# Two attention layers over four batches: first heads' slots filled from SBUF, products moved into the fills

## The chip, the cores and the metric

The kernel runs on one core of one Trainium2 chip. The metric is the device time of one execution in microseconds (us), as the median of several runs of the same program on the same inputs.

## What is computed

Two cross-attention layers run one after the other on `x` (4 batches, 512 queries, 320 channels) and a context `ctx` (4 batches, 512 tokens, 512 features), with 20 heads of width 16. In the first layer each head attends to the first 77 tokens (`text`) and to the other 435 (`ip`) with weights and softmaxes of their own. In the second layer the text is the first 508 tokens and `ip` the last 4, and the scores on the 4 tokens get a cosine between the averaged context `qsem` and each of the 4 tokens.

```
# first layer, each head
out = softmax(q k_text^T * s) v_text + softmax(q k_ip^T * s) v_ip
x = out @ Wo^T + bo + x
# second layer, each head
probs = softmax(q k_text^T * s)
qsem = l2norm(probs @ text);  sem = qsem @ l2norm(ip)^T
probs_ip = softmax(q k_ip^T * s + 0.5 * sem) * mask
x = (probs @ v_text + probs_ip @ v_ip) @ W_out + b_out + x
```

## The kernel before

Every engine runs a program of its own; counting semaphores join them, and nothing schedules but the order in which the code is written. A batch has four stages: the first layer's heads, a stretch of products between the layers, the second layer's heads, a stretch of products before the next batch. Batches 0, 1 and 2 are one `Fori` loop (`run_batches`), batch 3 is written out behind it, so there are two jumps back, at the ends of batches 0 and 1.

**Products.** `JOBS` lists the products of the stretches. Each goes to one PSUM bank of a ring of four (`ps_s`, `ps_t`), and ScalarE ("A") or VectorE ("D") frees it. Into the second layer they are `k1`, `tr0` (heads' outputs transposed), `x1` (output projection and residual), `q1`, then `g` (four blocks of `ctx^T ctx`, the Gram matrix from which `qsem`'s norm comes) and `v1` (four blocks of values). Into the next first layer they are `k0`, `q0`, `v0t` and `v0i` (values), `tr1` and `y` (output and residual).

**Slots.** Keys and queries go to TensorE in two parts, high and low, to keep fp32 accuracy. ScalarE's `high` and VectorE's `low` write the parts to SBUF, SyncE's `store` writes them to DRAM (`parts_k`, `parts_q`), and `load_slots` reads each head back, 48 rows at a time, into one of four slots (`k_slot`, `q_slot`). `split_and_loaded` does all that for one layer: it waits for all three row blocks of `k` and stores them, the same for `q`, waits until all is stored, and loads heads 0 to 3, then 4 to 19 as slots come free.

**Heads.** `run_heads` is a pipeline of three heads. `step(n)` makes the scores of head n+2 with their maxima, the transposed scores and exponentials of head n+1, and uses those of head n. Steps -2 and -1 are the fill: they have no head to use, so each hand-over (scores on TensorE, maximum on VectorE, bias on GpSimd, exponential on ScalarE) is waited for. The second layer's `step1` multiplies each head's exponentials with the Gram matrix (`ps_w<-gram,...`); before its step 0 TensorE waits for the copies in `before_use`, and ScalarE issues the next batch's loads (`context_done`).

## Time and profile before

| | us |
|---|---|
| median of three runs | 1805.31 (1803.68 to 1805.6) |
| the profiled execution | 1810.82 |
| its span, first to last instruction | 1809.0 |
| TensorE busy in the span | 1635.4 |
| VectorE, ScalarE, GpSimd busy | 1272.7, 1116.1, 463.6 |
| mean granted TensorE clock | 0.96 of full |

In the profile, times of instructions are counted from the span's start. Busy matmul time includes the tail of each matmul, which overlaps the next. The granted clock is 1.0 or 0.5 of full speed at any moment.

### The profile page before, as it was taken

The numbers are of one execution on the slowest core, as the hardware profiler recorded it, in microseconds if no ns is written. First come the engines' busy times: TensorE is split into PE (matmuls) and PEld (weight loads), VectorE is DVE, ScalarE is ACT, GpSimd is POOL, SyncE is SP. The second block draws the span as 40 slices with busy tenths as digits, with TensorE's granted clock in tenths as the row PEclk, the third lists the DMA queues.
The fourth block names the chain that finished last, engine by engine and source line by source line (L and its number), as shares of the span: only waits on it lengthen the run. The fifth ranks groups of instructions, "written<-read, shape, count | busy, mean of one in ns | idle before, by whom it ended". The sixth has DMA issues, their size and how long they took to land.

```text
span 1809.0 us, 34075 instructions
## 1 busy us (share of the span) xinstructions
PE 1635.4 (90%) x8608; PEld 1234.2 (68%) x8608; DVE 1272.7 (70%) x3548; ACT 1116.1 (62%) x2323; POOL 463.6 (26%) x1225
## 2 busy tenths in 40 slices
PE   5788989999978898999988888999998889999993
PEld 2455469999445447999835544999974554799991
DVE  2487358887678717888758853788875883588875
ACT  1599157776279627777429943677734991577760
POOL 0244013232025302323104411222301540233220
PEclk9899989999989998999989999999998999899996
DMA  7210220000301031001030111100012102100000
GB/s 234 75 35 22 88 65 21 19 18 20 114 29 35 13 104 53 22 17 32 1 121 31 35 48 61 59 20 17 28 45 85 35 26 79 36 18 21 17 20 15
DMA packets 47284, 83.04 MB, mean 46 GB/s; under 512 B 4417, under 2 KB 11857, under 8 KB 47185
## 3 DMA queue, kind: packets, MB, share of 16 engines
q1 hardware_dynamic: 43040, 74.15, 12.5%
q10 hardware_dynamic: 4144, 7.76, 1.4%
q8 instruction: 40, 0.66, 0.2%
q14 instruction: 60, 0.48, 0.1%
HBM read 47.78 MB, written 34.10 MB: 45 GB/s over the span
## 4 chain that ended last, share of the span: by engine, by line
PE 77%; ACT 10%; issue 5%; DVE 5%; DMA 1%; POOL 1%; ACTq 1%; SPq 0%; POOLq 0%; DVEq 0%
PE ps_w L838 37%; PE ps_s L838 17%; PE ps_t L838 16%; PE ps_b L838 4%; ACT probsT_high L461 4%; ACT probsT L469 4%; DVE row_max L648 2%; PE ps_m L838 2%; ACT q_slot L454 1%; ACT probs L495 1%; POOL probsT_low L383 1%; ACT probs L478 0%; ACT probs L536 0%; DMA w_ki<-in_wki 0%; DVE row_max L679 0%
## 5 line engine op out<-in xcount | busy, mean ns | idle before, releaser
L637 DVE TENSOR_TENSOR probsT_low<-probsT,probsT_high 128x512 fp32r<-128x512 f32 x560 | 394.1, 704 | 85.2 <-ACT probsT L469 76.0
L461 ACT ACTIVATE probsT_high<-ps_t 128x512 fp32r<-128x512 f32 x640 | 382.6, 598 | 113.9 <-PE ps_t L838 109.9
L838 PE MATMUL ps_w<-gram,probsT_high 128*128 128x416 f32 (+2 forms) x1280 | 390.8, 316 | 0.0
L469 ACT ACTIVATE probsT<-ps_t 128x512 f32<-128x512 f32 x640 | 384.0, 600 | 0.0
L838 PE MATMUL ps_w<-gram_low,probsT_high 128*128 128x384 f32 (+2 forms) x1280 | 354.5, 305 | 0.0
L495 ACT ACTIVATE probs<-ps_s,exp_bias 128x508 f32<-128x508 f32 x320 | 220.9, 691 | 125.9 <-POOL exp_bias L394 82.6
L838 PE MATMUL ps_s<-k_slot,q_slot 96*128 96x512 f32 x640 | 249.6, 434 | 32.0 <-issue 13.0
L838 PE MATMUL ps_t<-q_slot,k_slot 98*128 98x512 f32 x640 | 266.1, 435 | 11.0 <-ACT q_slot L454 9.2
L394 POOL TENSOR_SCALAR exp_bias<-row_max 128x1 f32<-128x1 f32 x320 | 129.7, 405 | 551.8 <-DVE row_max L679 551.8
L838 PEld LDWEIGHTS ps_w<-gram_low,probsT_high 128*128 128x128 f32 (+1 forms) x1280 | 244.8, 191 | 11.1
L838 PEld LDWEIGHTS ps_w<-gram,probsT_high 128*128 128x128 f32 (+1 forms) x1280 | 243.2, 190 | 11.5
L838 PE MATMUL ps_w<-gram,probsT_low 128*128 128x400 f32 (+2 forms) x1280 | 247.0, 315 | 0.0
L679 DVE TENSOR_REDUCE row_max<-ps_s 128x1 fp32r<-128x508 f32 x320 | 216.4, 677 | 0.0
L838 PEld LDWEIGHTS ps_w<-gram,probsT_low 128*128 128x128 f32 (+1 forms) x1280 | 214.4, 191 | 0.0
L696 DVE CUSTOM_DVE_ANT_0 probs<-ps_w,probs 128x380 f32<-128x380 f32 x320 | 174.0, 544 | 0.0
L648 DVE TENSOR_REDUCE row_max<-ps_s 128x2 fp32r<-128x870 f32 x160 | 168.2, 1051 | 0.0
L838 PEld LDWEIGHTS ps_t<-q_slot,k_slot 98*128 98x128 f32 x640 | 124.6, 196 | 58.3 <-ACT probsT L469 22.5
L838 PEld LDWEIGHTS ps_s<-k_slot,q_slot 96*128 96x128 f32 x640 | 119.7, 200 | 65.0 <-issue 28.0
L383 POOL TENSOR_TENSOR probsT_low<-probsT,probsT_high 128x512 fp32r<-128x512 f32 x80 | 103.6, 1295 | 164.2 <-ACT probsT L469 164.2
L454 ACT ACTIVATE q_slot<-ps_m 2x512 fp32r<-2x512 f32 x160 | 93.7, 586 | 79.1 <-PE ps_m L838 67.3
L695 DVE COPY head_out<-ps_w 128x36 f32<-128x36 f32 x320 | 62.3, 195 | 103.7 <-PE ps_w L838 103.6
L371 POOL CAST v_slot<-v_sb 128x16 fp32r (+3 forms) x160 | 63.8, 431 | 278.6 <-ACT probs L478 125.1
(153 smaller groups left out, 2056.9 us busy)
## 6 DMA issues: line engine op xcount, KB each, us to landing
q_slot<-parts_q SPq DMA_DIRECT2D x160, 96.0 KB
k_slot<-parts_k SPq DMA_DIRECT2D x160, 96.0 KB
parts_k<-probsT_high SPq DMA_DIRECT2D x24, 512.0 KB, 4.2
parts_q<-probsT_low SPq DMA_DIRECT2D x24, 512.0 KB, 4.3
parts_k<-probsT_high SPq DMA_DIRECT2D x24, 128.0 KB, 3.8
parts_q<-probsT_low SPq DMA_DIRECT2D x24, 128.0 KB, 3.6
ctx_sb<-in_ctxT ACTq DMA_DIRECT2D x3, 1024.0 KB, 8.3
vip_rep<-vip_rows SPq DMA_DIRECT2D x16, 160.0 KB, 3.6
```

Source lines behind the costliest of these rows:

```text
L371: last = nc.gpsimd.tensor_copy(v0_slot[par][:, blocks, cols], src)
L383: nc.gpsimd.tensor_tensor(probsT_low[1 - par][:, TB - 1, :], probsT[:, TB - 1, :], probsT_high[1 - par][:, TB - 1, :].bitcast(F32), ALU.su ...
L394: nc.gpsimd.tensor_scalar_mul(exp_bias[par][:, c:c + 1], row_max[1][par][:, c, 0:1].bitcast(F32), -SCALE)\
L454: nc.scalar.activation(q_slot[(k + 1) % SLOTS][SHIFT_ROW:ALL_ROWS, :], ps_m[0:SHIFT_ROWS, :], ACT.Copy)\
L461: nc.scalar.activation(probsT_high[1 - par][:, t, :], ps_t[:, t % 2, :], ACT.Exp, scale=SCALE)
L469: nc.scalar.activation(probsT[:, t, :], ps_t[:, t % 2, :], ACT.Exp, scale=SCALE).then_inc(pt_block[l], 1)
L495: nc.scalar.activation(probs[par][:, c, 0:TEXT1], ps_s[:, c % 2, 0:TEXT1], ACT.Exp, bias=exp_bias[par][:, c:c + 1], scale=SCALE, accum_out ...
L637: nc.vector.tensor_tensor(probsT_low[1 - par][:, t, :], probsT[:, t, :], probsT_high[1 - par][:, t, :].bitcast(F32), ALU.subtract).then_in ...
L648: nc.vector.tensor_reduce(out=row_max[0][par][:, cs, SHIFT_ROWS - 1:SHIFT_ROWS], in_=ps_s[:, :, TEXT0:T], axis=AX.X, op=ALU.max).then_inc( ...
L679: nc.vector.tensor_reduce(out=row_max[1][par][:, c, 0:1], in_=ps_s[:, c % 2, 0:TEXT1], axis=AX.X, op=ALU.max).then_inc(max_chunk, 1)
L696: nc.vector.tensor_tensor_reduce(out=probs[par][:, c, P:TEXT1], in0=ps_w[c % 2][:, 0:GN], in1=probs[par][:, c, P:TEXT1], scale=1.0, scalar ...
L838: return nc.tensor.matmul(out, lhsT, rhs, start=start, stop=stop)
```

## The change

In `split_and_loaded`, SyncE handles each row block by itself: as soon as row block 0 of `k` or `q` (the channels of heads 0 to 7) is split, twelve DMAs of 16 rows copy the parts of heads 0 to 3 from SBUF into the slots (`first_heads`), then the blocks are stored one by one. Only heads 4 to 19 are read from DRAM. `q1`'s parts get buffers of their own (`x_sb` and `out_all`), since `probsT_low` is written in the fill; for the first layer ScalarE and VectorE wait in step -1 for the stores of `k0` and `q0` instead.

On TensorE, the products `g` and `v1` stand inside the second layer's fill. Those of `v0t`, `v0i`, `tr1` and `y` stand inside the next first layer's fill (`fill0`), which is now at the end of a batch, ahead of the jump back. These products use a second ring, `ps_w0`, `ps_w1`, `ps_b`. The copies on ScalarE and VectorE move with them, GpSimd prepares head 0's values behind the fill (`gram_ready`), and SyncE instead of ScalarE issues the stores of the outputs.

```diff
+LATE = [("g", i) for i in range(TB)] + [("v1", t) for t in range(TB)] + [("ipn", 0), ("vip", 0)]
+BETWEEN = [("v0t", 0)] + [("v0i", t) for t in range(TB)] + [("tr1", m) for m in range(CBN)] + [("y", m) for m in range(CBN)]
...
+RING_NEXT = {("k0", 0): 2, ("k0", 1): 3, ("k0", 2): 0, ("q0", 0): 1, ("q0", 1): 2, ("q0", 2): 3}
+RING_BEFORE = {("q0", 1): ("k0", 0), ("q0", 2): ("k0", 1)}
...
+        parts["q1"] = [x_sb[:, :, :].bitcast(F32R),
+                       out_all[:, 0:CBN * S].rearrange("p (k s) -> p k s", k=CBN).bitcast(F32R)]
...
+        late_ring = [ps_w[0][:, :], ps_w[1][:, :], ps_b[:, :]]
+        late = {job: late_ring[i % len(late_ring)] for i, job in enumerate(LATE)}
+        late.update({job: late_ring[i % len(late_ring)] for i, job in enumerate(BETWEEN)})
...
+        def fill0(step, batch, b=FIRST):
+
+
+
+            step(batch, -2, SLOTS - 2, -1, False, False, True, b)
+            step(batch, -1, SLOTS - 1, -1, False, True, True, b)
+
+        def run_heads0(step, eng, b):
+
+            with eng.Fori(0, TURNS - 1) as turn:
+                for k in range(SLOTS):
+                    step(b, SLOTS * turn + k, k, turn, True, True, True)
+            for k in range(SLOTS):
+                step(b, HEADS - SLOTS + k, k, TURNS - 1, True, k < SLOTS - 1, k < SLOTS - 2)
...
-            def store(b, name):
+            def store(name, m):
                 for i, part in enumerate(ROW_PARTS[name[0]]):
-                    dst = scratch[name][i, :, :, :].rearrange("h d s -> (h d) s")
-                    src = parts[name][part].bitcast(F32)
-                    sp.dma_start(dst[0:2 * P, :].rearrange("(k p) s -> p k s", p=P), src[:, 0:2, :]).then_inc(stored[name], 16)
-                    sp.dma_start(dst[2 * P:C, :], src[0:CB[2], 2, :]).then_inc(stored[name], 16)
+                    dst = scratch[name][i, :, :, :].rearrange("h d s -> (h d) s")[P * m:P * m + CB[m], :]
+                    sp.dma_start(dst, parts[name][part].bitcast(F32)[0:CB[m], m, :]).then_inc(stored[name], 16)
+
+            def first_heads(l, name):
+
+                for k in range(SLOTS):
+                    slot = (q_slot if name[0] == "q" else k_slot)[k]
+                    for i, part in enumerate(ROW_PARTS[name[0]]):
+                        sp.dma_start(slot[PART * i:PART * i + PART, :].bitcast(F32),
+                                     parts[name][part].bitcast(F32)[D * k:D * k + D, 0, :]).then_inc(slots_in[l][k], 16)
...
-            def load_all(b, l):
-                with sp.Fori(0, TURNS) as turn:
-                    for k in range(SLOTS):
-                        load_slots(b, l, SLOTS * turn + k, k)
-
             def split_and_loaded(b, batch, l, names):
                 for name in names:
-                    wait_freed(sp, b, name, CBN - 1)
-                    store(b, name)
+                    for m in range(CBN):
+                        wait_freed(sp, b, name, m)
+                        sp.sem_inc(passed, 1)
+                        if m == 0:
+                            first_heads(l, name)
+                        store(name, m)
+                if l == 0 and b is not FIRST:
+                    store_outputs(b)
                 for name in names:
                     sp.wait_ge(stored[name], STORES * (batch + 1))
                 sp.sem_inc(passed, 1)
-                load_all(batch, l)
+                with sp.Fori(0, TURNS - 1) as turn:
+                    for k in range(SLOTS):
+                        load_slots(batch, l, SLOTS * turn + SLOTS + k, k)
+
+            def store_outputs(b):
+                for m in range(CBN):
+                    wait_freed(sp, b, "y", m)
+                    sp.sem_inc(passed, 1)
+                    sp.dma_start(outT[b, m * P:m * P + CB[m], :], x1_sb[0:CB[m], m, :]).then_inc(y_out, 16)
...
+                run_heads0(step0, pool, b)
+                def gram_ready():
+
+                    pool.wait_ge(stored["q1"], STORES * (b + 1))
+                    wait_freed(pool, b, "v1", TB - 1)
+                    pool.sem_inc(passed, 1)
+                    values_of(b, 0, 0)
+                    wait_freed(pool, b, "g", TB - 1)
+                    pool.sem_inc(passed, 1)
+                    for i in range(TB):
+                        lo = P * max(i, 1) - P
+                        nc.gpsimd.tensor_copy(gram[1][:, i, lo:GA], gram[0][:, i, lo:GA])
+                    values_of(b, 1, 1)
+
+                run_heads(step1, pool, b, gram_ready)
...
+                if transposed and not use:
+                    act.wait_ge(stored["k0"], STORES * (b + 1))
...
+                first, second = not use and not transposed, not use and transposed
                 if transposed:
                     shift(b, 1, n, k)
+                if second:
+                    gram_rows(b, 2)
+                    act.wait_ge(stored["k1"], STORES * (b + 1))
                 for c in range(SC):
                     if transposed:
                         expT(b, 1, n, par, c)
                     if scores and c < 2:
                         exps(c)
+                    if second and c == 0:
+                        gram_rows(b, 3)
+                    if second and c < TB - 1:
+                        v1_rows(b, c)
+                if first:
+                    gram_rows(b, 0)
                 if scores:
                     exps(2)
                     exps(3)
+                if first:
+                    gram_rows(b, 1)
+                if second:
+                    v1_rows(b, 3)
...
 
                 if scores:
                     maxima(0)
+                if outputs:
+                    output(last, 0)
+                if transposed and not use:
+                    dve.wait_ge(stored["q0"], STORES * (b + 1))
                 if transposed:
                     lowT(b, 0, n, par, 0)
                 if scores:
                     maxima(1)
+                if outputs:
+                    output(last, 1)
                 if transposed:
                     lowT(b, 0, n, par, 1)
+                if outputs:
+                    output(last, 2)
                 if use:
 
                     dve.wait_ge(o_done, HEADS * b + n + 1)
...
+                first, second = not use and not transposed, not use and transposed
+                output = second and last is not FIRST
                 if scores:
                     scores_half(0)
+                if first:
+                    values0(last)
+                if output:
+                    wait_freed(pe, last, "tr1", CBN - 1)
+                    by_channels(last, "y", "o1", heads_outT, (0,))
...
                     scoresT_of(0, g, k, 1)
+                if output:
+                    by_channels(last, "y", "o1", heads_outT, (1,))
...
+                if output:
+                    by_channels(last, "y", "o1", heads_outT, (2,))
+                if first and last is not FIRST:
+                    transposed_heads(last, "tr1", 1)
                 if scores:
```

**TensorE, into the second layer.** These are the last block of `q1` and what follows it, before the change (`ps_t<-x_sb,w_q` is `q1`, `<-ctx_sb` alone is `g`, `w_v` is `v1`, `k_slot,q_slot` are scores).

```order
L838 MATMUL ps_t<-x_sb,w_q 64x512 x3
L838 MATMUL ps_s<-ctx_sb 128x512 x4
L242 REGISTER_ALU
L838 MATMUL ps_s<-ctx_sb 128x384 x4
L242 REGISTER_ALU
L838 MATMUL ps_t<-ctx_sb 128x256 x4
L242 REGISTER_ALU
L838 MATMUL ps_t<-ctx_sb 128x128 x4
L242 REGISTER_ALU
L838 MATMUL ps_s<-w_v,ctx_sb 128x320 x4
```

The same place on TensorE after the change:

```order
L931 MATMUL ps_t<-x_sb,w_q 64x512 x3
L978 REGISTER_ALU
L1087 ISA
L931 MATMUL ps_s<-k_slot,q_slot 128x512
L1087 REGISTER_ALU
L931 MATMUL ps_s<-k_slot,q_slot 128x512
L931 MATMUL ps_w<-ctx_sb 128x512 x4
L1087 REGISTER_ALU
L931 MATMUL ps_s<-k_slot,q_slot 128x512
L1087 REGISTER_ALU
L931 MATMUL ps_s<-k_slot,q_slot 128x512
L931 MATMUL ps_w<-ctx_sb 128x384 x4
```

The scores of head 0 come directly behind `q1`, and the Gram blocks between them; the value blocks follow in step -1 in the same way.

**TensorE, into the next first layer.** These are the end of `q0` (`x_sb,w_q`) and the rows up to the jump back: `w_v` and `w_vi` are values, `ident,probsT` is `tr1`, `probs,w_o` is `y`.

```order
L838 MATMUL ps_t<-x_sb,w_q 64x512 x3
L242 REGISTER_ALU
L838 MATMUL ps_s<-w_v,ctx_sb 77x320 x4
L242 REGISTER_ALU
L838 MATMUL ps_s<-w_vi,ctx_sb 128x320 x4
...
L838 MATMUL ps_s<-probs,w_o 128x512 x3
...
L838 MATMUL ps_t<-probs,w_o 64x512 x3
L242 REGISTER_ALU
L252 REGISTER_ALU
L252 COMPARE_AND_BRANCH
L838 MATMUL ps_s<-k_slot,q_slot 128x512 x4
L838 MATMUL ps_m<-ident_r,row_max 2x128 x4
```

The same place on TensorE after the change:

```order
L931 MATMUL ps_t<-x_sb,w_q 64x512 x3
...
L995 ISA
L931 MATMUL ps_s<-k_slot,q_slot 128x512 x2
L931 MATMUL ps_w<-w_v,ctx_sb 77x320 x4
L931 MATMUL ps_w<-w_vi,ctx_sb 128x320 x4
...
L931 MATMUL ps_s<-k_slot,q_slot 128x512 x2
...
L1194 MATMUL ps_b<-ident,probsT 128x128 x4
...
L931 MATMUL ps_b<-probs,w_o 128x512 x3
...
L931 MATMUL ps_t<-q_slot,k_slot 128x512
...
L931 MATMUL ps_w<-probs,w_o 128x512 x3
...
L931 MATMUL ps_w<-probs,w_o 64x512 x3
...
L263 COMPARE_AND_BRANCH
```

The scores of the new batch's first heads stand ahead of the values, the transposes and outputs stand between them, and the jump comes behind the fill.

**SyncE, into the next first layer.** These are the stores and loads between the second layer's last load and the first layer's loop of loads.

```order
L312 DMA parts_k<-probsT_high 128x2x512
L313 DMA parts_k<-probsT_high 64x512
...
L312 DMA parts_q<-probsT_low 128x2x512
L313 DMA parts_q<-probsT_low 64x512
...
L334 ISA
...
L321 DMA q_slot<-parts_q 48x1x512
L321 DMA k_slot<-parts_k 48x1x512
```

The same place on SyncE after the change:

```order
L344 DMA k_slot<-probsT_high 16x512 x12
L337 DMA parts_k<-probsT_high 128x512 x3
...
L344 DMA q_slot<-probsT_low 16x512 x12
L337 DMA parts_q<-probsT_low 128x512 x3
...
L377 DMA outT<-x_sb 128x512
...
L367 ISA
...
L351 ISA
L353 ISA
```

The copies to the slots stand ahead of each name's stores, so `q`'s first copy comes behind 21 issues for `k`; the stores of the output stand ahead of the wait for `parts_k` and `parts_q`.

## Rows read from the trace of the kernel before

**Rows 1.** Windows: us, busy time per engine, PEclk, DMA share, GB/s.

```profile
682.00:690.00 8.00, 6.90 (x21) 4.29 (x22) 5.62 (x13) 6.29 (x15) 1.77 (x5) 0.53 0.00 0
705.00:865.00 160.00, 160.00 (x1055) 153.38 (x1054) 136.04 (x496) 120.12 (x266) 48.35 (x152) 1.00 0.07 22
965.00:1000.00 35.00, 30.15 (x153) 18.90 (x152) 31.43 (x52) 33.19 (x64) 17.23 (x32) 1.00 0.11 36
```

**Rows 2.** Timeline, TensorE, a steady second-layer head: start, length, [idle before <- what ended it].

```profile
701.49 1.10 PE L838 MATMUL ps_b<-gram,probsT 128*128 128x128 f32 x8
...
704.47 0.44 PE L838 MATMUL ps_t<-q_slot,k_slot 98*128 98x512 f32 x1
```

**Rows 3.** Timeline, TensorE, first to second layer, batch 1.

```profile
656.25 6.28 PE L838 MATMUL ps_s<-ctx_sb 128*128 128x512 f32 x16
...
674.37 0.73 PE L838 MATMUL ps_s<-k_slot,q_slot 96*128 96x512 f32 x2 [0.60 <-ACT v_sb L551]
...
681.89 0.50 PE L838 MATMUL ps_t<-q_slot,k_slot 98*128 98x512 f32 x1 [1.42 <-ACT q_slot L454]
...
687.46 2.07 PE L838 MATMUL ps_b<-gram,probsT 128*128 128x128 f32 x8
...
694.12 0.50 PE L838 MATMUL ps_t<-q_slot,k_slot 98*128 98x512 f32 x1 [1.01 <-ACT q_slot L454]
```

**Rows 4.** Timeline, TensorE, first to second layer, last batch.

```profile
1548.47 0.73 PE L838 MATMUL ps_s<-k_slot,q_slot 96*128 96x512 f32 x2 [0.53 <-ACT v_sb L551]
...
1566.84 0.44 PE L838 MATMUL ps_t<-q_slot,k_slot 98*128 98x512 f32 x1
```

**Rows 5.** Timeline, TensorE, into the next first layer, batches 1 to 2.

```profile
914.02 2.38 PE L838 MATMUL ps_s<-w_v,ctx_sb 128*77 128x320 f32 x8
...
927.17 6.00 PE L838 MATMUL ps_s<-probs,w_o 128*128 128x512 f32 x12 [0.85 <-ACT probs L536]
...
941.08 1.21 PE L838 MATMUL ps_s<-k_slot,q_slot 96*128 96x512 f32 x2 [5.05 <-issue]
...
952.19 1.22 PE L838 MATMUL ps_s<-k_slot,q_slot 96*128 96x512 f32 x2
...
958.85 0.72 PE L838 MATMUL ps_s<-k_slot,q_slot 96*128 96x512 f32 x2
```

**Rows 6.** Timeline, TensorE, into the last batch, whose code is unrolled.

```profile
1377.35 0.70 PE L838 MATMUL ps_s<-k_slot,q_slot 96*128 96x512 f32 x2 [1.16 <-DVE x_sb L818]
...
1395.10 0.71 PE L838 MATMUL ps_s<-k_slot,q_slot 96*128 96x512 f32 x2
```

**Rows 7.** Timeline, VectorE, batches 1 to 2.

```profile
898.55 0.69 DVE L631 TENSOR_TENSOR probsT_high<-ps_t,probsT_high 128x512 fp32r<-128x512 f32 x1 [0.74 <-ACT probsT_high L448]
...
911.53 0.68 DVE L631 TENSOR_TENSOR probsT_low<-ps_s,probsT_low 128x512 fp32r<-128x512 f32 x1
...
922.96 1.49 DVE L815 TENSOR_TENSOR probsT<-probs 128x1280 f32<-128x1280 f32 x1
```

**Rows 8.** Tile k_slot, SyncE queue: issues, ns min/median/max; then us to landing.

```profile
L321 SPq DMA_DIRECT2D k_slot<-parts_k x160: 713/722/802, 55.1 to 1719.1; - x160
L291 SPq DMA_DIRECT2D k_slot<-ip_shift x4: 574/586/667, 8.8 to 10.8; - x4
...
DMA to landing us min/median/max: 1.7/1.7/1.8
```

**Rows 9.** Tile parts_q: 64-row store issues, ns; us to landing.

```profile
L313 SPq DMA_DIRECT2D parts_q<-probsT_low x24: 479/495/1242, 46.2 to 1536.0; - x24
...
DMA to landing us min/median/max: 2.9/4.0/4.9
```

**Rows 10.** Timeline, SyncE queue, start of the program.

```profile
35.24 0.59 SPq L306 DMA_DIRECT2D mask_sb<-in_mask  x1
```

**Rows 11.** Timeline, TensorE, first fill.

```profile
44.29 2.38 PE L838 MATMUL ps_s<-w_v,ctx_sb 128*77 128x320 f32 x8
...
78.01 0.71 PE L838 MATMUL ps_s<-k_slot,q_slot 96*128 96x512 f32 x2
```

More of the change, by code:

```diff
@@ L360, in _, with step0 @@
                                     pattern=[[-1, P]], channel_multiplier=1).then_inc(built, 1)
[L362 removed]
+            def step0(b, n, k, turn, use, transposed, scores, last=FIRST):
                 par = k % 2
@@ L704, in step1 @@
                         maxima(c)
-                    if not use and not transposed and c == 1:
-                        ip_context(b)
+                    if first and c % 2 == 1:
+                        gram_lows(b, c // 2)
                     if use and c == 3:
@@ L823, in batch @@
                     link(b, nc.vector.memset(dump[:, 8:9], 0.0))
+                if ahead:
+                    fill0(step0, b + 1, b)
+                else:
+                    for m in range(CBN):
+                        output(b, m)
             lows(FIRST, "k0")
             lows(FIRST, "q0")
+            fill0(step0, 0)
             run_batches(dve, batch)
@@ L885, in head_maxT, with step0 @@
                 last.then_inc(maxT_done[l], 1)
-            def step0(b, n, k, turn, use, transposed, scores):
+            def step0(b, n, k, turn, use, transposed, scores, last=FIRST):
                 par = k % 2
@@ L974, in scores_of @@
                     scores_chunk((k + 2) % SLOTS, c, ps_s[:, c % 2, :]).then_inc(s_chunk, 1)
+                first, second = not use and not transposed, not use and transposed
                 if use:
@@ L998, in step1 @@
                     scores_of(1)
-                if not use and not transposed:
-                    ip_context(b)
+                if first:
+                    gram_of_context(b, 0)
+                if second:
+                    by_keys(b, "v1", "v1", 1)
                 if use:
```

186 lines of the change are left out of this document (106 added, 80 removed).

## The prediction, as put on record

> **What bounds the kernel now.** I read the windows first, then TensorE's timeline through each stretch between two layers, then the queues that feed it. In the middle of the second layer TensorE is busy 160.00 of 160 us, at the full clock (2.4 GHz); in the first layer's heads it is busy 30.15 of 35 us, the rest being short waits for other engines [rows 1]. The change touches neither: the same matmuls stand in every head. What it can move is the stretches around the fills. In the one into the second layer, products on the context run from 656.25 to 674.37, then the fill goes from 674.37 to 687.46, with idle times of which one of 1.42 is shown, and the granted clock is 0.53 from 682 to 690, so nearly all of that at the lower level, 1.2 GHz [rows 1, 3]. In the one into the next first layer, TensorE sits idle 5.05 us with nothing to wait for in the profile ("issue") before the first scores [rows 5]. That idle time is at the jump back of the batch loop: where the code is unrolled, at the last batch, it is 1.16 us, and ends with VectorE's output copy [rows 6]. So some 4 us of it belong to the jump; I use 4.3, as the output copy ends 0.75 us behind the last matmul, at 936.8.
>
> **Into the second layer, four times.** The products (17.5 us net of the last wait) and the fill are now one piece. Before, the fill took 687.46 - 674.37 = 13.1 us [rows 3]. I take 3.7 us of it as idle (the 1.42 shown, the rest smaller waits for maxima and exponentials) and half of the 3.9 us of matmuls at the low clock behind 682, 1.9 us, as lost to the clock; 7.5 us are work. The product blocks, of 1 to 3.5 us each, now stand in each of those waits. One wait is new: head 0 needs TensorE's last `vip` product copied, about 0.7 us. That makes 656.25 + 17.5 + 7.5 + 0.7 = 682.0 for the start of step 0, against 687.46. From there a steady head takes 704.47 - 701.49 = 3.0 us to its first transposed scores [rows 2]; before, at the low clock, it took 694.12 - 687.46 = 6.7, 1.01 of it waiting for ScalarE, which was still issuing the next batch's loads [rows 3]. ScalarE's queue issues them at the same place, so I keep 1.0: the scores come at 686.0, 8.1 us earlier. The last batch has no loads to issue: there the same piece took 1566.84 - 1548.47 = 18.4 us instead of 19.75, without the wait, so it gains 8.1 - 1.4 + 1.0 = 7.7 [rows 3, 4]. Four stretches: 3 x 8.1 + 7.7 = 32.0. Bounds: with only the 3.7 + 1.9 us of waiting and clock in the fill halved and the low clock kept in head 0, 3 us each (12); with no wait for ScalarE at all, 9 us each (36).
>
> ScalarE and VectorE get the Gram and value copies into a place where they were mostly waiting. GpSimd waits for `q1`'s stores behind the fill, some 15 us after their last issue, against landings of 2.9 to 4.9 us [rows 9], so that costs nothing. If the stores were later than that, the wait would hold head 0's values and TensorE with them.
>
> **What the slots cost.** The scores can start only when 16-row copies from SBUF have landed, and these stand in SyncE's one queue. None is in the trace. The nearest issues: a single row from SBUF to a slot takes 586 ns at the median, a 64-row store 495, a 48-row load from DRAM 722 [rows 8, 9]. I take 0.6 us, near the single row, which has the same source and target. Landing: the single row 1.7 us, a store 4.0 at the median [rows 8, 9]; I take 2.0, since source and target are those of the single row. [...] With 4.0 us instead, each fill that waits for its slot loses 2 us more.
>
> Into the second layer `k1` is long stored when `q1` comes, and the first queries' three issues and landing (1.8 + 2.0) fit in `q1`'s last two blocks of 3 us each. Into the next first layer it is closer. `k0`'s first block is split at 898.55 + 0.69 = 899.2; 12 copies and 9 stores at 0.6 keep the queue to 911.8; `q0`'s first block is split at 912.2, since VectorE has it between long operations [rows 7]; three issues and the landing give 916.0. TensorE has ended `q0` at 914.02 [rows 5]. It waits 2.0 us, and everything in its queue with it: the values, the transposes, the outputs.
>
> **Into the next first layer, batches 0 and 1.** Without that wait, values, transposes and outputs take from 914.02 to 941.08 - 5.05 = 936.0 [rows 5], of which 0.85 before the output is a wait that the fill now covers: 21.1 us. The fill's own work at the full clock is 12 score matmuls and 8 small ones, about 4.6 us; 1.3 us for waits of maxima and the last output copy. 914.0 + 2.0 + 21.1 + 4.6 + 1.3 = 943.0. VectorE's chain ends with 922.96 + 1.49 = 924.45 [rows 7] and serves the first maxima before TensorE has ended the values, so it doesn't hold. Then comes the jump, 4.3 us, not hidden by anything since all engines stand at it: step 0 starts at 947.3, against 952.19 [rows 5]. Before, the low clock that followed the idle time lay on the fill and the start of step 0, which took 958.85 - 952.19 = 6.7 us instead of about 5.4. Now it lies on steps full of matmuls, where half the clock costs more: I charge 3.5 us (0 if the clock holds, 7 if it is low for three heads). Gain: 4.9 + 1.3 - 3.5 = 2.7 us, twice, 5.4. Bounds of one: -3 to +7.
>
> **Into the last batch.** No jump: 943.0 is 6.2 us later than the last output copy before (936.8), which there ends at about 1377.1, just ahead of the first scores, so the heads can start at 1383.3. Before, step 1 started at 1395.10, so step 0 at the full clock would have begun at 1389.7 [rows 6]. That is 6.4; I take 5.5, for some low clock after the 2 us wait.
>
> **The first fill.** SyncE is busy with weight loads until 35.24 + 0.59 = 35.8 [rows 10]. 21 issues give 48.4, three more and the landing 52.2. TensorE has ended `q0` at 44.29 [rows 11], so it sits idle 7.9 us, then does the values (some 11 of the 12.3 us up to the output's wait in the later stretch [rows 5], part of it at the low clock) and the fill: step 1 starts near 81.5, against 78.01 [rows 11]: -3.5. Bounds: -8 to 0.
>
> **Sum.** 32.0 + 5.4 + 5.5 - 3.5 = 39.4 us off. The profiled execution took 1810.8 us, its span 1809.0; the median of the runs, 1805.3, is 0.3% lower, and I apply the sum to it: 1766 us. What moved at no cost is the issue of the outputs' stores from ScalarE to SyncE: they stand in front of SyncE's wait for the stores and of head 4's load, and that head's scores come two heads, 11 us, later.
>
> **Rivals.**
> - *Slower issues* (or landings): at 0.72 us for each 16-row copy and store, the 24 issues from `k0` to the first slot end 2.9 us later, against 0.4 us of room. With three such fills and 3 to 4 us at the first, 12 us are lost: 1778. A landing of 4.0 us does 8 of that alone.
> - *Other side:* the same queue, from about 1.0 us an issue. Then each of four fills loses 24 x 0.4 = 10 us, and the 39 us are gone. The longest 64-row store took 1242 ns [rows 9]; if all issues took that, each fill would lose 24 x 0.64 = 15 us, and the time would be about 1827. Medians of 586 ns for one row and 495 for 64 rows speak against it [rows 8, 9].
> - *The low clock stays.* The 2 us wait for the queries comes in an otherwise full piece. The granted clock fell to half in 682 to 690 after idle times of this size [rows 1, 3]. If it falls here, 5 us are lost on the values and again behind the jump: three times 5 to 6, 1782. The Trainium skill, "TensorE: Matmul & The Clock Gate", section "Loop structure matters more than you think", warns of just this: a DMA wait in front of matmuls lets the clock drop. By it the last two cases would come together.
> - *No gain into the second layer*: the hand-overs on ScalarE, now with 12 copies more, set the fill's pace. Then the four stretches gain 3 us each, and the sum is 19: 1786. A first-layer head already keeps ScalarE at 33.19 of 35 us [rows 1], so it has little room in a steady stage; but in the fill the 17.5 us of products give it time for twelve copies that are smaller than its exponentials.
>
> **Chances.** The forecast 0.60 (1755 to 1774); the queue at 0.72 or the landing 0.13 (1774 to 1782); clock or ScalarE 0.16 (1778 to 1795); the queue from 1.0 us on, 0.04; all waits hidden, under 1755, 0.07. The range that leaves out no more than 2 in 10 is 1754 to 1787. Differences below 0.2% can't be told from none; within that I put 0.02, slower 0.04, faster 0.94.
>
> **What would show it.** In the changed profile: TensorE's first Gram product of a second layer some 26 us behind `q1` and a clock of 1.00 through it; first scores of a first layer about 2 us behind `q0`, ended by a landing; 16-row issues near 0.6 us; an idle time of 4 to 5 us behind the last maximum's transposes in batches 0 and 1 alone, with a low clock on the heads behind it. I am wrong if those issues take 1 us, if the products leave idle times between them, or if heads slow down elsewhere.

## The result, and the profile after

Four runs of each kernel on the same chip gave 1753.99 us (1752.99 to 1755.05) against 1804.49 us (1803.60 to 1805.60): a ratio of 0.972, 95% interval 0.970 to 0.974. That is 50.5 us off, where the forecast was 39.4. The profiled execution of before (1810.82 us) isn't among its four; that of after (1753.93 us) is. The sign and the mechanism held; the gains into both layers were put too small.

The page of the changed kernel, its head, and below it the windows (us, then busy time of each engine, granted clock, DMA share, GB/s) that answer to [rows 1] and to the two kinds of fill:

```profile
span 1752.1 us, 34255 instructions
PE 1601.0 (91%) x8608; PEld 1218.5 (70%) x8608; DVE 1271.6 (73%) x3548; ACT 1113.8 (64%) x2323; POOL 461.3 (26%) x1225
```

```profile
630.00:667.00 37.00, 35.08 (x121) 18.54 (x119) 14.03 (x34) 15.55 (x40) 4.94 (x18) 1.00 0.23 71
667.00:682.00 15.00, 15.00 (x103) 14.45 (x104) 11.22 (x46) 9.37 (x20) 3.25 (x11) 1.00 0.39 128
705.00:865.00 160.00, 160.00 (x1061) 153.69 (x1060) 134.31 (x496) 116.78 (x257) 47.58 (x151) 1.00 0.06 19
889.00:918.00 29.00, 27.19 (x92) 14.37 (x90) 19.14 (x34) 8.16 (x16) 1.65 (x8) 0.94 0.33 102
918.00:931.00 13.00, 7.58 (x31) 4.89 (x30) 5.75 (x10) 6.35 (x12) 2.62 (x5) 0.74 0.14 38
```

Read the head first. The same 8608 matmuls keep TensorE busy 34.4 us less than the 1635.4 us of before, out of 56.9 us by which the two profiled spans differ. The other 22.5 us are idle time. Most of the 34 us is clock: in the low stretches of the two traces TensorE was busy for 96.4 us before and for 33.5 after. A score matmul of 0.40 us (682.23 before) took 0.79 there (686.82), so half of the difference, 31 us, is an estimate of what the clock gave back. The remaining 3 us may be tails of matmuls, which overlap more when the matmuls stand closer; that isn't shown. The mean granted clock agrees: 0.96 leaves 0.04 x 2 x 1809.0 = 145 us at the lower level, 0.981 leaves 67. The second layer's fill and its start (630 to 682) are at 1.00 throughout; before, 682 to 690 had 0.53 [rows 1].

TensorE's timeline of the changed kernel, into the second layer of batch 1, answers to [rows 3]:

```profile
636.10 5.90 PE L931 MATMUL ps_t<-x_sb,w_q 128*128 128x512 f32 x12
641.92 0.74 PE L931 MATMUL ps_s<-k_slot,q_slot 96*128 96x512 f32 x2
642.50 3.60 PE L931 MATMUL ps_w<-ctx_sb 128*128 128x512 f32 x8
...
666.86 1.15 PE L931 MATMUL ps_b<-gram,probsT 128*128 128x128 f32 x8 [1.08 <-DVE vip L823]
...
669.89 0.44 PE L931 MATMUL ps_t<-q_slot,k_slot 98*128 98x512 f32 x1
```

Scores start with no wait behind `q1`: the slots have landed. From `q1`'s end to head 0's first transposed scores it now takes 669.89 - 641.92 = 27.97 us, and took 694.12 - 656.25 = 37.87: 9.9 us less, forecast 8.1. ScalarE's timeline at that place shows why head 0 no longer waits for it:

```profile
666.80 0.41 ACTq L297 DMA_DIRECT2D ctx_sb<-in_ctxT  x1
...
667.92 0.54 ACTq L301 DMA_DIRECT2D x_sb<-in_xT  x1
668.72 0.58 ACT L507 ACTIVATE q_slot<-ps_m 2x512 fp32r<-2x512 f32 x1 [5.48 <-PE ps_m L931]
```

Its three load issues begin at 666.80, just ahead of step 0 (666.86), and end at 668.46, before the shift row is wanted. Before the change they stood behind the last exponentials of the fill. They began 2.9 us behind step 0's start (687.46) and took 2.8 us:

```profile
690.38 0.43 ACTq L271 DMA_DIRECT2D ctx_sb<-in_ctxT  x1
...
690.97 1.23 ACTq L274 DMA_DIRECT2D x_sb<-in_xT  x1
692.36 0.79 ACTq L275 DMA_DIRECT2D x_sb<-in_xT  x1
693.41 0.58 ACT L454 ACTIVATE q_slot<-ps_m 2x512 fp32r<-2x512 f32 x1 [2.80 <-issue]
```

TensorE's timeline into the first layer of batch 2 answers to [rows 5], and SyncE's issues at the same place to [rows 8, 9]:

```profile
888.71 1.07 PE L931 MATMUL ps_t<-x_sb,w_q 64*64 64x512 f32 x2
891.52 0.72 PE L931 MATMUL ps_s<-k_slot,q_slot 96*128 96x512 f32 x2 [1.74 <-DMA q_slot<-probsT_low]
892.08 3.55 PE L931 MATMUL ps_w<-w_v,ctx_sb 128*77 128x320 f32 x8
...
917.69 0.40 PE L931 MATMUL ps_m<-ident_r,row_max 128*2 128x128 f32 x4
922.83 1.22 PE L931 MATMUL ps_s<-k_slot,q_slot 96*128 96x512 f32 x2 [4.74 <-issue]
...
929.91 0.71 PE L931 MATMUL ps_s<-k_slot,q_slot 96*128 96x512 f32 x2
```

```profile
875.70 6.94 SPq L344 DMA_DIRECT2D k_slot<-probsT_high  x11
882.68 5.34 SPq L337 DMA_DIRECT2D parts_k<-probsT_high  x9
888.20 8.28 SPq L344 DMA_DIRECT2D q_slot<-probsT_low  x12
```

The copies take SyncE 0.63 to 0.69 us from one to the next (forecast 0.6), the stores 0.59. The wait for the queries is 1.74 us here and in the last batch, 1.97 in batch 1 (forecast 2.0), the jump back 4.74 (forecast 4.3). In the very first fill the wait is 9.11 us (forecast 7.9) and step 1 starts at 80.42 (forecast 81.5, before 78.01 [rows 11]):

```profile
52.87 1.22 PE L931 MATMUL ps_s<-k_slot,q_slot 96*128 96x512 f32 x2 [9.11 <-DMA q_slot<-probsT_low]
```

To compare kernels I cut the trace at step 0's first transposed scores and at each layer's end; "first step 0" is the time of these scores in batch 0's first layer. "Into second layer" is from a first layer's end to the second layer's step 0; "into first layer" from a second layer's end to the next step 0. From the traces, in us:

| kernel | first step 0 | into second layer, batches 0 to 3 | into first layer, three |
|---|---|---|---|
| before | 73.5 | 71.2, 72.8, 72.9, 69.6 | 60.7, 60.5, 56.0 |
| after | 76.0 | 62.9, 61.3, 61.3, 61.1 | 54.1, 55.4, 50.7 |
| e1 first side ahead | 76.1 | 61.4, 61.3, 62.9, 61.1 | 59.4, 60.0, 56.1 |
| e2 second side ahead | 76.1 | 75.7, 75.7, 75.7, 73.7 | 54.1, 53.7, 49.4 |
| e3 slots alone | 70.6 | 74.5, 74.0, 73.6, 73.5 | 59.7, 60.0, 56.1 |
| e4 slots from DRAM | 79.4 | 73.9, 74.7, 76.1, 74.8 | 67.2, 67.2, 62.6 |
| e5 second side, products put right | 76.4 | 73.0, 74.4, 74.4, 72.3 | 55.6, 55.4, 50.7 |
| e6 slots alone, products put right | 70.4 | 73.2, 74.3, 72.9, 72.6 | 59.7, 59.3, 55.6 |
| e9 slots alone, cleanly | 70.1 | 71.1, 71.7, 72.2, 68.3 | 59.2, 59.8, 56.0 |
| e13 second side, cleanly | 75.9 | 71.4, 72.2, 72.2, 71.3 | 53.9, 53.9, 49.0 |
| e10 before, with filler | 73.1 | 74.2, 72.7, 72.2, 70.3 | 60.3, 60.3, 55.6 |
| e7 unrolled | 75.2 | 61.1, 61.1, 61.1, 61.1 | 50.8, 48.8, 48.8 |
| e8 queries first | 71.4 | 61.3, 61.3, 61.3, 61.2 | 53.9, 53.4, 48.7 |
| e11 both | 71.3 | 61.1, 61.1, 61.1, 61.1 | 48.6, 48.6, 48.5 |
| e12 values split | 70.5 | 61.1, 61.1, 61.1, 62.8 | 47.9, 47.9, 47.9 |

### The profile page after: what moved, and what is told of

Its sections match the earlier page's. It is cut to its first block, busy times and chain, and to the rows that moved or that the text cites. A ratio compares the mean times of both kernels' runs of the same rounds, so it can differ in the third digit from the quotient of the medians.

```text
span 1752.1 us, 34255 instructions
## 1 busy us (share of the span) xinstructions
PE 1601.0 (91%) x8608; PEld 1218.5 (70%) x8608; DVE 1271.6 (73%) x3548; ACT 1113.8 (64%) x2323; POOL 461.3 (26%) x1225
## 4 chain that ended last, share of the span: by engine, by line
PE 75%; ACT 9%; issue 7%; SPq 4%; DVE 3%; POOL 1%; DMA 0%; ACTq 0%; POOLq 0%; DVEq 0%
PE ps_w L931 44%; PE ps_t L931 11%; PE ps_s L931 11%; PE ps_b L931 7%; ACT probsT_high L514 4%; ACT probsT L522 4%; DVE row_max L725 2%; SPq L344 2%; PE ps_m L931 2%; SPq L337 1%; SPq L309 1%; ACT probs L533 1%; POOL probsT_low L425 1%; PE ps_b L1058 0%; DMA q_slot<-probsT_low 0%
## 5 line engine op out<-in xcount | busy, mean ns | idle before, releaser
L706 DVE TENSOR_TENSOR probsT_low<-probsT,probsT_high 128x512 fp32r<-128x512 f32 x560 | 393.1, 702 | 83.5 <-ACT probsT L522 74.2
L931 PE MATMUL ps_s<-k_slot,q_slot 96*128 96x512 f32 x640 | 240.3, 418 | 29.9 <-DMA q_slot<-probsT_low 14.6
L931 PE MATMUL ps_t<-q_slot,k_slot 98*128 98x512 f32 x640 | 262.2, 427 | 1.0
L931 PE MATMUL ps_w<-probsT_high,v_slot 128*68 128x512 f32 x320 | 107.4, 416 | 9.1 <-ACT probsT L522 4.5
```

What stands on the lines that cost most here:

```text
L706: nc.vector.tensor_tensor(probsT_low[1 - par][:, t, :], probsT[:, t, :], probsT_high[1 - par][:, t, :].bitcast(F32), ALU.subtract).then_in ...
L931: return nc.tensor.matmul(out, lhsT, rhs, start=start, stop=stop)
```

## Experiments: which half brings it

The theory: products cover the fills' waits and so keep the clock up, and the copies from SBUF are what lets the first scores stand ahead of the products. The rivals: the copies alone bring it; the order alone brings it; or it is the clock alone. The runs were made on several chips, and the kernel before took 1806 to 1809 us beside them, so ratios to it (with 95% intervals) are compared, not times alone.

**e1.** The first layer's side undone. The edit on TensorE (VectorE's three outputs stand ahead of its fill likewise):

```diff
                 if ahead:
+                    values0(b)
+                transposed_heads(b, "tr1", 1)
+                wait_freed(pe, b, "tr1", CBN - 1)
+                by_channels(b, "y", "o1", heads_outT)
+                if ahead:
+                    wait_freed(pe, b, "y", CBN - 1)
                     fill0(step0, b + 1, b)
-                    wait_freed(pe, b, "y", CBN - 1)
-                else:
-                    transposed_heads(b, "tr1", 1)
-                    wait_freed(pe, b, "tr1", CBN - 1)
-                    by_channels(b, "y", "o1", heads_outT)
```

> The changed kernel with one part undone: values, transposed heads and outputs stand ahead of the next first layer's fill again, as in the kernel before; the very first fill and all second-layer fills stay changed. My theory (the products cover the waits of the fill): the stretches into the next first layer take what they took before, less nothing for the slots, since the copies from SBUF land behind products either way. They gained 6.6, 5.1 and 5.3 us with the heads' +1.6, +0.7, -1.1 beside them, so 14 to 17 us come back: 1768 to 1771. Rival, slots alone: if the gain there came from slots that are filled sooner, it stays and the time is 1754 to 1757. Rival, low clock: if moving the products only moved a low-clock stretch, under 5 us come back, 1755 to 1759.

Measured 1775.16 us, 0.983 (0.981 to 0.985): 1.1% of the time, some 20 us, comes back, a little more than expected. The three stretches take 59.4, 60.0 and 56.1 us, against 60.7, 60.5 and 56.0 before. The slots alone bring 1.3 us at most there.

**e2.** The second layer's side undone:

```diff
                 by_channels(b, "q1", "q1", x1_sb)
+                for i in range(TB):
+                    gram_of_context(b, i)
+                for t in range(TB):
+                    by_keys(b, "v1", "v1", t)
+                wait_freed(pe, b, "v1", TB - 1)
```

with the same calls taken out of `step1`, ScalarE's and VectorE's copies moved along, and the four-bank ring of before.

> The changed kernel with the other part undone: Gram and value products of the second layer stand ahead of its fill again, ip_context in its last step; the first-layer side stays changed. My theory: the four stretches into the second layer, 62.9, 61.3, 61.3, 61.1 us in the changed kernel, go back to 70 to 73 each, 32 to 42 us in all: 1786 to 1796. I expect ScalarE's wait for its load issues (1.0 us) and the low clock of the fill to come back with it. Rival, slots alone: the gain came from copying the first slots out of SBUF, and the time stays within 1754 to 1760.

Measured 1806.18, 1.000 (0.999 to 1.001): 50 to 52 us come back, not 32 to 42, and the stretches are 2.8 to 4.5 us longer than in the kernel before. So e2 had lost something that before had (e5, e13).

**e3.** e1 and e2 together, and the values ahead of the very first fill too.

> Only the SBUF copies of the first four heads are left of the change: all products stand ahead of the fills, in the first layer's first fill too. My theory: in the kernel before, no fill waited for a DMA except the very first one, so this is the time of before less what the first fill gains (2 to 5 us): 1798 to 1804. Rival, slots alone bring the gain: 1754 to 1770. Rival, the queue: 24 issues on SyncE in one piece delay the heads behind them, over 1806.

Measured 1814.25, 1.005 (1.003 to 1.007): slower than expected, and in the range of the queue rival. But the stretches into the first layer are at most 0.1 us longer than before; it is those into the second that are, by 0.7 to 3.9 us, as in e2. What that is, e5, e6 and e9 ask.

**e4.** The changed order with the first slots from DRAM:

```diff
-                        if m == 0:
-                            first_heads(l, name)
...
                 sp.sem_inc(passed, 1)
+                for k in range(SLOTS):
+                    load_slots(batch, l, k, k)
```

> The changed kernel's order of products with the slots of heads 0 to 3 filled from DRAM again, behind the stores. With e3 this makes the two-by-two table of copies and order. My theory: both parts need each other. The first scores stand ahead of the products and wait for nine stores, their landing (2.9 us), a load issue and its landing (2.5 us): 9 us more at three first-layer fills, 5 to 7 at four second-layer fills, 2 at the first: 45 to 57 us more, 1800 to 1811, so no gain over before is left. Rival, order alone: the products cover the round trip, 1754 to 1765.

Measured 1848.21, 1.024 (1.022 to 1.026). The direction is right, the size nearly double (94 us over the changed kernel). Its TensorE timeline into the second layer and into the next first one:

```profile
680.81 1.22 PE L931 MATMUL ps_s<-k_slot,q_slot 96*128 96x512 f32 x2 [11.04 <-DMA k_slot<-parts_k]
...
943.99 1.21 PE L931 MATMUL ps_s<-k_slot,q_slot 96*128 96x512 f32 x2 [13.02 <-DMA k_slot<-parts_k]
```

I had expected 5 to 7 and 9 us. The waits come with low clock behind them: TensorE's busy time is 1614.5 us against 1601.0. The order alone is worse than nothing. (The nine stores of a name take SyncE 5.3 us, the six of before took 4.6, so storing block by block isn't the cause.)

**e5, e6.** The kernels e2 and e3 had kept the two image-prompt products at the end of step -1, where nothing covers them any more. Here they are back in step -2:

```diff
                     scores_of(1)
                 if first:
-                    gram_of_context(b, 0)
-                if second:
-                    by_keys(b, "v1", "v1", 1)
+                    ip_context(b)
...
-                if second:
-                    by_keys(b, "v1", "v1", 3)
-                    ip_context(b)
```

> e2 again with one thing put right: e2 had left the two image-prompt products (norms and values of the last four context rows) at the end of step -1, where nothing covers them once the Gram products stand ahead; here they are back in step -2, between its second and third score block, as in the kernel before. My theory: e2's stretches into the second layer (75.7 us) held 3 to 4 us of that each, so they come to 72 to 73 us, and the time to 1790 to 1797, 36 to 43 us over the changed kernel. Rival: the place of the two products costs nothing and e2's 1806 stands, so that the waits of the changed SyncE and GpSimd queues cost it.

> e3 again with the image-prompt products in step -2 as in the kernel before, so that only the SBUF copies of the first four heads (and the buffers that they need) are left of the change. My theory: stretches into the second layer as before (70 to 73 us), into the next first layer 0.4 to 1.0 us shorter, first fill 2.4 us shorter as in e3: 1798 to 1803, a change of 0.1 to 0.4%. Rival, the copies cost what they bring: 1805 to 1810.

Measured 1807.01, 0.999 (0.998 to 1.000), and 1815.61, 1.005 (1.003 to 1.006). e5 is its rival; e6 lies even above its own. The stretches into the second layer fell by 1.3 to 2.7 us from e2 to e5, but the whole did not, since those into the first layer came out 1.3 to 1.7 us longer; no run says why. They are still 1.5 to 2.7 us above the kernel before. TensorE's timeline of e6 shows one thing that was missing, a wait that the products had covered:

```profile
688.46 0.74 PE L919 MATMUL ps_m<-ident_r,row_max 128*2 128x128 f32 x4
691.34 0.71 PE L919 MATMUL ps_w<-gram,probsT_high 128*128 128x416 f32 x1 [2.13 <-POOL gram L434]
```

In the changed kernel GpSimd splits head 0's values behind the fill. There TensorE doesn't wait for them; here, without products in the fill, it does.

**e9, e13.** So GpSimd's order of before goes with it:

```diff
-                if use and scores:
+                if scores:
                     values_of(b, n + 2, par)
...
-                    values_of(b, 0, 0)
...
-                    values_of(b, 1, 1)
```

> e6 once more with GpSimd's order of before as well: the Gram copies ahead of the fill and the two first heads' value splits within it, where e6 still had them behind it, so that TensorE waited 2.13 us for the first head's values in each second layer. Now only the copies from SBUF and their buffers are left. My theory: e6's into-second-layer stretches (73.0 to 74.3 us) lose 2 us each, and the time comes to 0.995 to 1.000 of the kernel before (1796 to 1805 where that takes 1805): the copies alone are worth only the first fill's 2 to 3 us. Rival, the copies' 24 issues on SyncE cost what they bring: 1.002 to 1.005.

> The changed kernel with the second layer's side undone cleanly: Gram and value products ahead of the fill, the two image-prompt products in step -2, and GpSimd's Gram copies and value splits where the kernel before has them (e5 had them behind the fill, with a wait of 2 us on TensorE). My theory: the products in the second layer's fills are worth what e9 and the changed kernel differ by in these four stretches, 8.2, 10.4, 10.9 and 7.2 us, 37 us in all, plus up to 2 us of low clock in the heads behind them: 1790 to 1794, a ratio to the kernel before of 0.990 to 0.993. Rival, e5 stands: the wait for GpSimd only hid another one, 0.997 to 1.000.

e9: 1806.22, 0.999 (0.998 to 1.000), as expected. e13: 1797.43 (1791.46 to 1800.15), 0.995 (0.993 to 0.997), slightly above what I had expected, and under the rival; its profiled execution, the fastest of six, has a span of 1789.7 us, 37.6 over the changed kernel's. From e6 to e9 the four stretches fell by 2.1, 2.6, 0.7 and 4.3 us, from e5 to e13 by 1.6, 2.2, 2.2 and 1.0. This gives a clean table, in ratios to the kernel before:

| | products ahead of fills | products in the fills |
|---|---|---|
| first slots from DRAM | 1 | 1.024 (e4) |
| first slots from SBUF | 0.999 (e9) | 0.972 |

Neither half brings anything alone. e9 also keeps the smaller parts of the change (stores block by block, `q1`'s own buffers, SyncE storing the outputs), so none of these is the gain. The products in the second layer's fills are worth 40.5 us in the four stretches (e13 against after: 8.5, 10.9, 10.9, 10.2).

## Experiments: the clock, the jump and the queue

**e10.** Is the clock alone the gain? The kernel before, with ten unused matmuls in the fill's waits:

```diff
+                def filler(count):
+                    for _ in range(count):
+                        mm(ps_w[1][:, :], x1_sb[:, 0, 0:P], x1_sb[:, 0, :], True, True)
...
                     head_maxT(1, 1 - par)
+                if second:
+                    filler(3)
```

> The kernel before, with ten 128x128x512 matmuls on data that are not used, put into the waits of each second layer's fill: three ahead of the maxima's wait, three behind the maxima's transposes, one behind each of four score blocks. Nothing else moves. It asks how much of the gain is the clock alone. TensorE was busy 1635.4 us before and 1601.0 after for the same 8608 matmuls, so by my present theory (the low clock is the greater part) 34 of the 57 us are matmuls at the low clock, brought on by the idle times of the fills. Theory A, filling the waits keeps the clock: the second layer's start stays at the full clock and each of the four stretches gains 1 to 4 us net of what the fillers themselves delay: 4 to 16 us off. Rival B, the clock falls for another reason (what ran ahead of the fill): the low stretch at 682 us stays, and the fillers cost 0 to 2 us each: 0 to 8 us more.

Measured 1813.49, 1.004 (1.003 to 1.006). The windows of the fill and of step 0, before (first fence) and with filler (second):

```profile
674.00:688.00 14.00, 9.83 (x34) 4.93 (x35) 7.03 (x19) 8.45 (x21) 2.66 (x10) 0.80 0.07 26
```

```profile
674.00:688.00 14.00, 13.27 (x48) 6.79 (x48) 5.45 (x15) 6.23 (x16) 2.43 (x9) 1.00 0.09 35
688.00:696.00 8.00, 5.75 (x31) 3.89 (x30) 4.82 (x18) 5.14 (x13) 1.39 (x5) 1.00 0.22 56
```

Theory A is right about the clock and wrong about the time. Where TensorE has no idle time in the fill, the low stretch of 10.2 us goes in all four batches (3.4 us are left in batch 0), and the mean clock of the kernel is 0.973 instead of 0.96. But the fillers, 0.9 us each and not the 0.45 that I had in mind, take what the clock gives back: step 0 starts at 690.42 instead of 687.46, and in it TensorE waits for ScalarE longer than before (1.01 us):

```profile
696.00 0.50 PE L838 MATMUL ps_t<-q_slot,k_slot 98*128 98x512 f32 x1 [2.10 <-ACT q_slot L454]
```

Useful products do both at once: they keep the clock and are gone from the path ahead of the fill. With smaller fillers the clock alone might gain; that wasn't tried.

**e7.** The batch loop written out on TensorE alone:

```diff
-            with eng.Fori(0, BATCH - 1) as b:
-                batch(b, True)
+            if eng is unrolled:
+                for b in range(BATCH - 1):
+                    batch(b, True)
```

> The changed kernel with the batch loop written out on TensorE alone; the loops over heads and all other engines' loops stay. My theory: the 4.74 us of idle time ahead of step 0 in batches 0 to 2's jumps go (two stand in a program with three loop passes, between batches 0, 1 and 2), and with them a low-clock stretch of 6.8 us behind each, worth about 1.5 to 2 us: 11 to 14 us off, 1740 to 1744. Rival, another engine's jump takes its place: all engines loop, and if ScalarE or VectorE stand as long at their own jumps, TensorE waits for them instead, and under 3 us go: 1751 or more. Rival, half: the idle time goes and the clock stays: 1744 to 1747.

Measured 1738.76, 0.961 (0.959 to 0.963), against 0.972: some 15 to 19 us, a little more than expected. TensorE's timeline at the old jump:

```profile
908.02 0.40 PE L935 MATMUL ps_m<-ident_r,row_max 128*2 128x128 f32 x4
909.23 0.72 PE L935 MATMUL ps_s<-k_slot,q_slot 96*128 96x512 f32 x2 [0.81 <-DVE x_sb L716]
```

Instead of 4.74 us of "issue" it waits 0.81 for the last output. The other engines still jump, and none of their jumps takes the place. The rest is mostly clock: TensorE is busy 1591.4 us, 9.6 less than in the changed kernel. The low stretches behind the two jumps are gone. The value blocks ahead of the jump ran at half clock for a while on the way into batches 2 and 3 of the changed kernel (the one at 892.08 took 3.55 us, not 2.32), here on the way into batch 1 alone (3.89).

**e8.** The queries' copies ahead of the keys' stores, at first layers only:

```diff
                 for name in names:
+                    wait_freed(sp, b, name, 0)
+                    sp.sem_inc(passed, 1)
+                    first_heads(l, name)
...
+                if l == 0:
+                    for name in names:
+                        for m in range(CBN):
+                            wait_freed(sp, b, name, m)
+                            sp.sem_inc(passed, 1)
+                            store(name, m)
```

> The changed kernel with one reordering on SyncE, at the first layer's fills only: the query copies into the first four slots are issued ahead of the nine stores of the keys, not behind them. My theory, the queue bounds the fill: the very first fill gains the stores' 5.4 us of the 9.1 us wait; the waits of 1.7 us at the next first-layer fills go where they are (three times at most): 5 to 10 us off, 1744 to 1749. Rival, it moves the wait: the keys' stores now land later and hold ScalarE's first exponentials, which wait for them, so that the gain is under 2 us or negative: 1752 to 1758.

Measured 1744.84, 0.965 (0.963 to 0.968), 8 to 12 us better than the changed kernel. The very first fill's wait falls from 9.11 to 2.75 us. At the others it falls only from 1.74 to 1.50:

```profile
885.86 0.72 PE L939 MATMUL ps_s<-k_slot,q_slot 96*128 96x512 f32 x2 [1.50 <-DMA q_slot<-probsT_low]
886.42 2.32 PE L939 MATMUL ps_w<-w_v,ctx_sb 128*77 128x320 f32 x8
```

So the keys' stores delayed those by 0.2 to 0.5 us only, and the 2 us gained in two of these stretches are again the value blocks at full clock (2.32).

**e11.** Both edits together.

> e7 and e8 together: TensorE's batch loop written out and the query copies ahead of the keys' stores. My theory: both gains add up, since they lie in different places (behind the fill, and ahead of it): e7 gave 15 to 19 us, e8 8 to 12, so 1726 to 1732, a ratio to the kernel before of 0.955 to 0.959. Rival, they share the low clock: the low stretches behind the first-layer fill are counted in both, 1733 to 1738.

Measured 1730.25 (1729.36 to 1732.42), 0.957 (0.955 to 0.958): they add up. By the ratios that is 1.6% under the changed kernel.

**e12.** One value block, or two in the first fill, ahead of the first scores.

```diff
+                if first:
+                    values0(last, range(0, 2 if last is FIRST else 1))
                 if scores:
                     scores_half(0)
```

> e11 with one more step: the first of the five value blocks stands ahead of the first scores (two of them in the very first fill), so that TensorE works while the query copies land. My theory: the waits of 1.5 to 1.9 us at the three first-layer fills go, and 3 to 4 us at the very first: 6 to 9 us less than e11, 1718 to 1725. Rival, the fill's chain over VectorE and ScalarE starts later by the block (2.3 us) and ends later by as much: within 2 us of e11.

Measured 1729.82, 0.957 (0.955 to 0.959): no different from e11. The waits for the queries are gone, but VectorE's timeline in the first fill shows what comes next:

```profile
65.96 0.69 DVE L718 TENSOR_TENSOR probsT_low<-probsT,probsT_high 128x512 fp32r<-128x512 f32 x1 [6.03 <-DMA parts_q<-probsT_low]
```

It may not overwrite the queries' split before their nine stores have landed, and those now stand at the end of SyncE's queue. At the three later fills 0.6 to 0.7 us each is gained, not 1.5 to 1.9: there TensorE now waits about 0.7 us for a maximum.

## Why the prediction was off

**Into the second layer: right mechanism, term too small.** The forecast was 3 x 8.1 + 7.7 = 32.0 us. The profiles show 8.3, 11.6, 11.6 and 8.5 in the stretches, and 1.9 more in batch 0's first heads, 41.8 in all. For batch 1, 9.9 of the 11.6 lie behind `q1`'s end, where I had 8.1. One step of the working failed there: "ScalarE's queue issues them at the same place, so I keep 1.0". The place in the program is the same, but in the changed fill ScalarE is done with its exponentials and copies at 663.2, ahead of step 0, and not behind its start. The issues began 0.06 us ahead of step 0 instead of 2.9 behind it, took 0.41, 0.39 and 0.54 us instead of 0.43, 1.23 and 0.79, and cost nothing: 1.0 us. The fill itself ended 666.86 - 641.92 = 24.9 us behind `q1`, where 25.7 was worked out: 0.8 us. The other 1.7 lie ahead of the fill: in the profile of before the clock was low for 3.4 us on `k1` in batches 1 and 2, in that of after in batch 0 instead. That the change has a part in this isn't shown. The 1.9 us in batch 0's heads are a second low stretch of before. So of the 9.8 us that this term was short, 6.2 lie behind `q1` (1.8 in each of three batches, 0.8 in the last), and 3.6 are low clock at places that the sum put at nothing (1.7 + 1.7 - 1.7 + 1.9). I had looked for low clock only in the fill and in head 0.

**Into the next first layer: only the charge for the clock failed.** Forecast 2.7, 2.7 and 5.5; measured, with the heads behind, 5.0, 4.4 and 6.3. From `q0`'s end to step 0 it took 922.83 - 889.78 = 33.1 us, worked out 33.3. But I charged 3.5 us for a low clock on steps that are full of matmuls. Step 0 took 929.91 - 922.83 = 7.1 us, 1.7 over the 5.4 of full clock. The low stretch behind the jump was 6.8 us long in the trace's clock records, against 17.1 before. The jump itself was read rightly, but not its reason ("all engines stand at it"): with TensorE's loop alone written out it is gone (e7).

**The first fill: right.** Forecast 3.5 us lost, measured 80.42 - 78.01 = 2.4 at step 1.

**Waits of the queue: right.** None of the rivals on SyncE's queue came: an issue is 0.6 to 0.7 us, and one wait in each first-layer fill is left. The first scores start 1.4 to 1.5 us behind the end of the third copy's issue (52.87 and 891.52, against 51.44 and 890.02), where I had taken 2.0 for the landing. Nor did the hand-overs on ScalarE set the fill's pace. The rival that the clock stays low came in small: a 1.74 us wait was followed by 3.4 us of low clock in two of three batches. That costs 1.7 us on the values, not the 5 to 6 that I had put on it with the stretch behind the jump. The Trainium skill, "TensorE: Matmul & The Clock Gate", section "Loop structure matters more than you think", warns of a long DMA wait between matmuls, with the clock low behind it. The trace agrees at the 9.11 us wait of the first fill, with 10.2 us of low clock from 46.5 on. The forecast's wait was 2 us, so "just this" said too much.

**The sum.** By the profiles these terms make 41.8 + 15.7 - 2.5 = 55.0 us off. Of the other 1.9 us between the two spans (56.9), 1.7 lie behind the last heads, where the output products ran longer at half clock before than after. The medians make 50.5. The profiled execution of before was 6 us above its median (clock 0.960; of the 57 runs of before in the experiments those with that clock took 1808.7 to 1811.6 us, those with 0.964 took 1802.2 to 1802.8), so its rows hold more low clock than a typical run. I read the terms from it and took the sum off the median, which hid part of the error. What I had not done is the one count that gives the whole: TensorE's busy time in the low stretches of before. Its half, 48 us, is an estimate of what all low clock cost, and would have been worth setting beside the 1.9 us a fill that I took. The measured 1753.99 falls into the case "all waits hidden, under 1755", which had 0.07, but not for its reason: the waits for the queries were not hidden.

**Still open.** In the changed kernel the value blocks lose the clock behind waits of 1.74 us twice and keep it behind one of 1.97. In e7 they lose it behind 2.12 and keep it behind 1.85 and 1.86. In e8 and e11 (six waits of 1.46 to 1.62 us) they keep it. The length of the wait alone doesn't decide it; what does, no run here tells.

## What to carry to other kernels

Split a gain between two layers of a pipeline into idle time and clock before it is forecast: half of the time in which TensorE is busy at the low clock bounds the second part, and it may be the larger. Two edits that look separable (where data come from, what stands in front) brought 2.8% together; alone, the first brought nothing that can be told from noise and the second cost 2.4%. An undo is clean only when the other engines' orders go back with it: a GpSimd step that was free behind a long fill cost 0.7 to 4.3 us a layer, about 2 on average, behind a short one.

## What the runs showed of the hardware

- At the jump back of the batch loop TensorE stood 5.05 and 5.29 us with nothing to wait for in the profile before, 4.74 and 4.90 after, and 3.6 at the least in the other kernels with that jump (e6, e9). Written out it is 0.8 us (e7) to 1.2 us (the last batch of before), which an output copy on VectorE explains; the other engines' jumps were hidden.
- In the second layer's fill of before, idle times of 0.6 to 1.4 us on TensorE were followed by a granted clock of 1.2 GHz for 10.2 us; with those waits filled it stayed at 2.4 GHz (e10). The stretches full of matmuls behind a wait or a jump were back at 2.4 GHz after 3.4 to 6.8 us (after), the sparse fills of before after 10 to 17.
- A 16-row copy from SBUF to SBUF (32 KB) takes SyncE 0.63 to 0.69 us from one to the next, a store of one block 0.59, and a 48-row load from DRAM 0.70 to 0.81 for its issue (e4).
- With the stores and reloads in the queue, the first scores of a fill waited 10.7 to 13.3 us (e4). With the copies they waited for no DMA into the second layer, 1.7 to 2.0 us into the next first layer, and 9.1 in the very first fill.
